# A softmax division moved to each head's output, in an attention stage of a two-layer kernel

## The chip, the cores and the metric

The kernel runs on one core of a Trainium2 chip. The metric is the device time of one execution in microseconds (us). Engines: TensorE (PE, its weight loads PEld), VectorE (DVE), ScalarE (ACT), GpSimd (POOL), and the sync engine SyncE (SP), which issues DMAs.

## The reference

Two layers on x of 2 x 512 x 1024. The first is cross attention with 32 query heads and 8 key/value heads of width 128 over a context of 2 x 1024 x 1024; behind it come a routed bias, a fake-quantised product and a gated feed-forward net. Only the attention's core is touched by the change:

```python
q = _apply_rope(q, curr_seq_pos)
k = _apply_rope(k, curr_seq_pos)
raw = jnp.einsum('bhqd,bhkd->bhqk', q, k) / scale
masked = raw + mask[:bs, None, curr_seq_pos:curr_seq_pos + sq, :sk]
attn = jax.nn.softmax(masked, axis=-1)
out = jnp.einsum('bhqk,bhkd->bhqd', attn, v)
out = out.transpose((0, 2, 1, 3)).reshape(bs, sq, N_Q_HEADS * D_V)
return out @ wo
```

Shapes here: 2 batches, 512 queries, 1024 keys.

## The kernel before

The program is a row of stages with a barrier between them: projections of queries, keys and values into DRAM (`q_d`, `k_d`, `v_d`), then `attention_stage`, which writes each head's transposed output to `o_d`, then `output_stage` and the rest. The change edits `attention_stage` alone, apart from one scratch array that `build` hands to it.

The stage walks over 2 batches x 32 heads x 4 quarters of 128 queries: 256 steps. Step n of the text is one quarter; four steps are a head, 16 steps a group of four heads that share a K and a V tile. All fp32 products are done as three products of high and low halves (`split_matmul`, L117 to L119), so that every operand is there as a high half (copied by ScalarE) and a low half (raw minus high: by GpSimd for Q, K, V, tiles at_ql, at_kl, at_vl; by VectorE for the probabilities, at_ptl).

Each engine has its own program, written out by hand, with the same loop: in step n it does the actions of the steps n minus a lag.

- TensorE: scores of step n (6 matmuls into at_s), transposes of step n-2 (8 into at_t, L1001), a quarter of the mixing with V of step n-6 (6 matmuls into at_o).
- VectorE: in step n `mask_and_max` (a memset of at_turnstile, then the fused add of the mask and row maximum, at_sc<-at_s, L952, then the negation, L955); for step n-1 `normalise` (reciprocal, L959, and the multiplication of the 128x1024 probabilities at_pr in place, L961); for step n-2 `turn_low` (at_ptl, L968, twice 128x512).
- ScalarE: the high halves of Q, K, V when due, `turn_high` of step n-2 (at_pth, L905), the exponential of step n with its row sum (at_pr, L895), and per head `copy_out` (at_ot<-at_o, L911) in step 4h+10 and `store_out` (a DMA to `o_d`, L916) in step 4h+11.
- GpSimd: the low halves of Q (step 4h-3), K (8 steps ahead of its group) and V (6 steps ahead).
- SyncE: the loads of Q, K and V at the same step numbers, each after a wait that its raw buffer is free.

The first LEAD = 12 steps are written out; then, for each batch, a loop of three passes over 32 steps, and the fourth pass written out again. So there are four returns of a loop in the stage, and each engine has its own.

Buffers: two each for at_s, at_sc, at_pr and at_ot; at_t has two halves, one for each four transposes. TensorE's transposes of step n-2 wait for `normed` (L961's event) and for the half of at_t to be free, which at_ptl of the step before frees.

Of the kernel before, what the change touches and what calls it, by code (L numbers as in the profile page):

```python
# [19 lines left out]
F32 = mybir.dt.float32  # L20
# [5 lines left out]
P = 128  # L26
# [7 lines left out]
QT = SQ // P  # L34
# [683 lines left out]
def attention_stage(nc, q_d, k_d, v_d, o_d, mask, ident):  # L718
# [8 lines left out]
    with ExitStack() as ctx:  # L727
# [18 lines left out]
        sm = sb("sm", [P, 2, 4], F32)  # L746
        turnstile = sb("turnstile", [P, 1], F32)
# [7 lines left out]
        o_st = [sem("o_st0"), sem("o_st1")]  # L755
        k_hi, v_hi, q_hi = event("k_hi"), event("v_hi"), event("q_hi")
# [4 lines left out]
        maxed = event("maxed")  # L761
        expd = event("expd", 2)
        recipd = event("recipd")
        normed = event("normed")
# [16 lines left out]

        def at(b, i, h):

            if isinstance(i, int):
                return b + (i * HP + h) // HQ, (i * HP + h) % HQ
            return b, i * HP + h

        MIX_LAG = QT + 2
        COPY_LAG = MIX_LAG + QT
        STORE_LAG = COPY_LAG + 1  # L790
        LEAD = STORE_LAG + 1

# [24 lines left out]
        def _(sp):  # L817
            def fetch(b, i, kind, x):
# [5 lines left out]
                elif kind == "v":  # L824
                    bb, h = at(b, i, x * GRP)
                    start = h // GRP * DH if isinstance(i, int) else i * (KG * DH) + x * DH
                    sp.wait_ge(v_lo.sem, v_lo.free(group(b, i, x), 1))
                    sp.dma_start(vraw[:], v_d[bb].rearrange("t p n -> p t n")[:, :, bass.ds(start, DH)]).then_inc(v_in, 16)
                else:
                    bb, h = at(b, i, x)  # L830
                    sp.wait_ge(q_lo.sem, q_lo.free(head(b, i, x), 2))
                    sp.dma_start(qraw[:, x % 2], q_d[bass.ds(h, 1)].rearrange("a p n -> p (a n)")[:, bb * SQ:(bb + 1) * SQ]).then_inc(q_in[x % 2], 16)

            def do_step(b, i, n):
                for kind, x in fetches(b, i, n):
                    fetch(b, i, kind, x)


# [8 lines left out]
            program(sp, do_step)  # L847

        @block.gpsimd
        def _(pool):  # L850
# [10 lines left out]

            def do_step(b, i, n):
                for kind, x in fetches(b, i, n):
                    fetch(b, i, kind, x)

            k_lo.open(pool)
# [7 lines left out]
        def _(act):  # L874
# [38 lines left out]
            def store_out(b, i, h):  # L913
                bb, hh = at(b, i, h)
                act.wait_ge(copied.sem, copied.done(head(b, i, h)))
                act.dma_start(o_d[bass.ds(hh, 1)].rearrange("a p n -> p (a n)")[:, bb * SQ:(bb + 1) * SQ],  # L916
                              ot[:, h % 2]).then_inc(o_st[h % 2], 16)

            def do_step(b, i, n):
# [6 lines left out]
                for lag, act_on in ((COPY_LAG, copy_out), (STORE_LAG, store_out)):  # L926
                    if (n - lag) % QT == 0 and exists(b, i, n - lag):
                        act_on(b, i, (n - lag) // QT)
# [3 lines left out]
            for s in range(2):  # L932
                act.sem_inc(o_st[s], 16)
# [3 lines left out]
            for s in range(2):  # L937
                act.wait_ge(o_st[s], 16 * (B * HQ // 2 + 1))

        @block.vector  # L940
        def _(dve):
            def mask_and_max(b, i, n):
# [3 lines left out]
                elif b == 0 and isinstance(i, int) and i == PASSES - 1 and n == NS:  # L946
# [28 lines left out]
            masked.open(dve)  # L975
            t_lo.open(dve)
# [3 lines left out]
        def _(pe):  # L980
# [14 lines left out]
            def turn(b, i, n):  # L995
                pe.wait_ge(normed.sem, normed.done(step(b, i, n)))
# [862 lines left out]
def build(nc, x, context, mask, wq, wk, wv, wo, router_w, router_b, expert_b, s1, z1, s2, z2,  # L1859
# [6 lines left out]
    v_d = scratch("v_d", (B, KT, P, D))  # L1866
    o_d = scratch("o_d", (HQ, DH, T))
# [31 lines left out]
    with ExitStack() as ctx:  # L1899
# [21 lines left out]
        attention_stage(nc, q_d, k_d, v_d, o_d, mask, ident)  # L1921
# [45 lines left out]
```

## Time and profile before

| | us |
|---|---|
| median of 3 runs | 3474.62 |
| lowest and highest run | 3468.10, 3477.11 |
| the profiled execution | 3472.4 |
| its span | 3470.6 |
| attention stage in it, about | 1000 to 1973 |

The page's first part, busy time, share of the span and instructions of each engine:

```profile
PE 3020.7 (87%) x14144; PEld 2418.9 (70%) x14144; DVE 2881.7 (83%) x4335; ACT 2154.2 (62%) x2742; POOL 911.7 (26%) x547
```

How to read the rows further below. In the view of stretches the columns are: the stretch, its length, then PE, PEld, DVE, ACT, POOL busy us with the number of instructions, the granted TensorE clock as a share of full speed, the DMA share, GB/s. In a timeline a row is: start us, duration us, engine, line, operation, written tile<-read tiles, shapes, how many were merged, and in brackets the engine's idle time ahead of it with what ended it. In the view of a line or tile: how many, duration in ns as min/median/max, first and last start. In the view of waits: who waited for whom, us in total, times, the longest. "issue" is time in which the engine waited for nothing that the profile shows. Ends of matmuls are modelled, and they are pipelined.

### The profile page before, as it was taken

What the parts mean: (1) busy time and instruction counts of PE and PEld (TensorE: products, weight loads), DVE (VectorE), ACT (ScalarE), POOL (GpSimd) and SP (SyncE); (2) the same over time, 40 slices, a digit from 0 to 9 for tenths busy, and PEclk for the clock granted to TensorE, in tenths of its full rate; (3) what the DMA queues carried; (4) which work ended last, traced back from release to release, by engine and by line L of the source; (5) the groups of instructions that cost most, each with busy time, mean ns of one, the idle gap of its engine ahead of it and who ended that gap; (6) DMA issues with size and microseconds to landing.
All of it is one profiled execution on the core that took longest, in us unless ns stands there. A gap on an engine that the chain in (4) does not pass through costs nothing. (4 is left out here: it accounts for less than half of the span.)

```text
span 3470.6 us, 45684 instructions
## 1 busy us (share of the span) xinstructions
PE 3020.7 (87%) x14144; PEld 2418.9 (70%) x14144; DVE 2881.7 (83%) x4335; ACT 2154.2 (62%) x2742; POOL 911.7 (26%) x547
## 2 busy tenths in 40 slices
PE   5888858687769999999999799995656999999999
PEld 4777746566648888888888677774425777777787
DVE  7999969679769999999999799997574788888753
ACT  4777747567657777777777588884142565655531
POOL 3777746226121111111111055550000101101100
PEclk8999979899989999999999899997577999999999
DMA  3333432342331111111111233420022221212211
GB/s 110 128 113 116 132 133 91 123 138 91 127 119 56 55 52 55 46 62 49 58 49 49 103 122 121 133 97 31 0 97 66 68 67 61 85 61 67 73 49 52
DMA packets 170400, 286.81 MB, mean 83 GB/s; under 512 B 11776, under 2 KB 98816, under 8 KB 170240
## 3 DMA queue, kind: packets, MB, share of 16 engines
q1 hardware_dynamic: 161024, 268.24, 23.3%
q10 hardware_dynamic: 9216, 16.78, 1.3%
q8 instruction: 58, 0.95, 0.1%
q14 instruction: 102, 0.84, 0.1%
HBM read 196.64 MB, written 88.34 MB: 82 GB/s over the span
## 5 line engine op out<-in xcount | busy, mean ns | idle before, releaser
L905 ACT ACTIVATE at_pth<-at_t 128x512 fp32r<-128x512 f32 x512 | 281.9, 596 | 249.3 <-PE at_t L1001 249.3
L205 ACT ACTIVATE ff_nf_above<-ff_nf_raw,sharp 128x1024 f32<-128x1024 f32 x255 | 291.6, 1148 | 92.5 <-DVE ff_nf_val L220 72.9
L952 DVE CUSTOM_DVE_ANT_0 at_sc<-at_s,at_mk 128x1024 f32<-128x1024 f32 x256 | 312.1, 1219 | 29.9 <-issue 9.5
L968 DVE TENSOR_TENSOR at_ptl<-at_t,at_pth 128x512 fp32r<-128x512 f32 x512 | 328.1, 682 | 1.1 <-ACT at_pth L905 1.1
L220 DVE SCALAR_TENSOR_TENSOR ff_nf_val<-ff_nf_above,ff_nf_val 128x1024 f32<-128x1024 f32 x238 | 308.2, 1295 | 21.2 <-ACT ff_nf_above L205 18.6
L205 ACT ACTIVATE pq_nf_above<-pq_nf_raw,sharp 128x1024 f32<-128x1024 f32 x240 | 263.2, 1113 | 99.3 <-DVE pq_nf_val L220 84.0
L205 ACT ACTIVATE ou_nf_above<-ou_nf_raw,sharp 128x1024 f32<-128x1024 f32 x240 | 267.3, 1117 | 77.8 <-DVE ou_nf_val L220 62.4
L895 ACT ACTIVATE at_pr<-at_sc,at_sm 128x1024 f32<-128x1024 f32 x256 | 295.3, 1154 | 14.7 <-DVE at_sm L955 7.9
L1001 PE MATMUL at_t<-ident,at_pr 128*128 128x128 f32 x2048 | 272.5, 274 | 20.1 <-DVE at_ptl L968 19.0
L117 PE MATMUL ff_g<-yT_h,ff_guh 128*128 128x512 f32 x704 | 286.6, 407 | 0.0
L1001 PEld LDWEIGHTS at_t<-ident,at_pr 128*128 128x128 f32 x2048 | 234.7, 140 | 71.4 <-DVE at_ptl L968 27.8
L220 DVE SCALAR_TENSOR_TENSOR pq_nf_val<-pq_nf_above,pq_nf_val 128x1024 f32<-128x1024 f32 x224 | 274.3, 1224 | 8.6
L220 DVE SCALAR_TENSOR_TENSOR ou_nf_val<-ou_nf_above,ou_nf_val 128x1024 f32<-128x1024 f32 x224 | 273.2, 1220 | 5.8
L119 PE MATMUL ff_g<-yT_h,ff_gul 128*128 128x512 f32 x704 | 276.3, 392 | 0.0
L118 PE MATMUL ff_g<-yT_l,ff_guh 128*128 128x512 f32 x704 | 274.6, 390 | 0.0
L117 PE MATMUL pq_pj<-xT_h,pq_wh 128*128 128x512 f32 x512 | 209.6, 409 | 55.5 <-POOL pq_wl L483 55.5
L117 PE MATMUL ou_acc<-ou_wh,ou_oh 128*128 128x512 f32 x512 | 210.4, 411 | 36.2 <-DVE X L1168 18.1
L860 POOL TENSOR_TENSOR at_ql<-at_qraw,at_qh 128x512 fp32r<-128x512 f32 x64 | 82.0, 1281 | 573.1 <-ACT at_qh L890 573.1
L961 DVE TENSOR_SCALAR at_pr<-at_pr,at_sm 128x1024 f32<-128x1024 f32 x256 | 218.8, 855 | 9.1
L117 PE MATMUL at_s<-at_kh,at_qh 128*128 128x512 f32 x512 | 201.7, 394 | 25.3 <-POOL at_ql L860 25.3
L117 PE MATMUL at_o<-at_pth,at_vh 128*128 128x512 f32 x512 | 221.8, 433 | 0.2 <-DVE at_ptl L968 0.2
L197 POOL TENSOR_TENSOR ff_nf_raw<-ff_nf_raw,ff_nf_am 128x1024 f32<-128x1024 f32 x17 | 39.5, 2321 | 690.5 <-DVE ff_nf_am L192 690.5
(210 smaller groups left out, 8105.5 us busy)
## 6 DMA issues: line engine op xcount, KB each, us to landing
ff_raw<-dq SPq DMA_DIRECT2D x63, 512.0 KB, 4.0
pq_raw<-in_L_xattn_wq SPq DMA_DIRECT2D x32, 512.0 KB, 5.1
q_d<-pq_res SPq DMA_DIRECT2D x32, 512.0 KB, 2.6
at_qraw<-q_d SPq DMA_DIRECT2D x64, 256.0 KB, 2.7
o_d<-at_ot ACTq DMA_DIRECT2D x64, 256.0 KB, 2.0
ou_oraw<-o_d SPq DMA_DIRECT2D x32, 512.0 KB, 3.8
ou_wraw<-in_L_xattn_wo SPq DMA_DIRECT2D x32, 512.0 KB, 4.1
pq_nf_raw<-in_L_ffn_w SPq DMA_DIRECT2D x16, 512.0 KB, 5.4
```

Of the source, the lines that this page charges most:

```text
L117: pe.matmul(out, w[0], x[0], start=start, stop=False)
L118: pe.matmul(out, w[0], x[1], start=False, stop=False)
L119: return pe.matmul(out, w[1], x[0], start=False, stop=stop)
L205: act.activation(self.above[:, (s + j) % 2, 0:width], self.raw[:, s, 0:width], ACT.Relu, bias=self.sharp[:, j:j + 1], scale=SHARP).then_in ...
L220: dve.scalar_tensor_tensor(v, above, STEPS[j], v, ALU.min, ALU.add).then_inc(self.stepped.sem, 1)
L860: pool.tensor_tensor(qq[1][:, x % 2], qraw[:, x % 2], f32(qq[0][:, x % 2]), ALU.subtract).then_inc(q_lo.sem, 1)
L895: act.activation(pr[:, n % 2], sc[:, n % 2], ACT.Exp, bias=sm[:, n % 2, 1:2], accum_out=sm[:, n % 2, 2:3]).then_inc(expd.sem, 1)
L905: act.activation(pt[0][:, h % 2, j * HALF:(j + 1) * HALF, (n % QT) * P:(n % QT + 1) * P], t_ps[:, j], ACT.Copy).then_inc(t_hi.sem, 1)
L952: dve.tensor_tensor_reduce(sc[:, n % 2], s_ps[:, n % 2], mk[:, bb * QT + n % QT], 1.0, NEG, ALU.add, ALU.max, sm[:, n % 2, 0:1]).then_inc( ...
L961: dve.tensor_scalar(pr[:, n % 2], pr[:, n % 2], sm[:, n % 2, 3:4], None, ALU.mult).then_inc(normed.sem, 1)
L968: dve.tensor_tensor(pt[1][sl], t_ps[:, j], f32(pt[0][sl]), ALU.subtract).then_inc(t_lo.sem, 1)
L1001: last = pe.transpose(t_ps[:, j, c, :], pr[:, n % 2, k * P:(k + 1) * P], ident[:])
```

## The change

The probabilities are no longer divided by their row sum before they are transposed. The exponential's row sums of a head's four quarters are gathered in `sums`; once per head VectorE inverts them (128x4) and transposes the inverses in blocks of 32x32 (`invert`). SyncE writes them to a small DRAM array `r_d` with four DMAs (`store_inverse`) and reads them back as one row of 512 for all 128 partitions (`load_inverse_row`); GpSimd multiplies the head's output at_ot by that row in place (`scale_out`), and SyncE, no longer ScalarE, stores it. The fused operation of the mask now makes the negated masked scores and their minimum, so that the negation of the maximum is gone, and the exponential takes a scale of -1. The transposes wait for `expd` instead of `normed`. In SyncE's order the stores of the inverses stand 8 steps, the row load 10 and the output's store 15 behind a head's first step; at the same step number the Q, K and V loads come first. LEAD is 16.

```diff
@@ attention_stage @@
-        sm = sb("sm", [P, 2, 4], F32)
-        turnstile = sb("turnstile", [P, 1], F32)
+        low = sb("low", [P, 2], F32)
+        sums = sb("sums", [P, 2, QT], F32)
+        inv = sb("inv", [P, 2, 32], F32)
+        invT = sb("invT", [P, 2, 32], F32)
+        inv_row = sb("inv_row", [P, 2, SQ], F32)
+        turnstile = sb("turnstile", [P, 2], F32)
...
-        STORE_LAG = COPY_LAG + 1
+        STORE_LAG = COPY_LAG + QT + 1
         LEAD = STORE_LAG + 1
+        INV_LAG = QT
+
+        INV_OUT_LAG = 2 * QT
+        ROW_LAG = INV_OUT_LAG + 2
...
+            def store_inverse(b, i, h):
+
+                sp.wait_ge(inv_turned.sem, inv_turned.done(head(b, i, h)))
+                for q in range(P // 32):
+                    sp.dma_start(r_d[h % 2].rearrange("(t q j) -> q t j", t=QT, j=32)[q],
+                                 invT[32 * q:32 * q + QT, h % 2]).then_inc(inv_out[h % 2], 16)
+
+
+            def load_inverse_row(b, i, h):
+                sp.wait_ge(inv_out[h % 2], written(b, i, h) + 64)
+                sp.dma_start(inv_row[:, h % 2], r_d[h % 2].rearrange('(a n) -> a n', a=1).broadcast_to((P, SQ))).then_inc(inv_in[h % 2], 16)
+
+            def store_out(b, i, h):
+                bb, hh = at(b, i, h)
+                sp.wait_ge(scaled.sem, scaled.done(head(b, i, h)))
+                sp.dma_start(o_d[bass.ds(hh, 1)].rearrange("a p n -> p (a n)")[:, bb * SQ:(bb + 1) * SQ],
+                             ot[:, h % 2]).then_inc(o_st[h % 2], 16)
+
             def do_step(b, i, n):
                 for kind, x in fetches(b, i, n):
                     fetch(b, i, kind, x)
-
+                for lag, act_on in ((INV_OUT_LAG, store_inverse), (ROW_LAG, load_inverse_row), (STORE_LAG, store_out)):
+                    if (n - lag) % QT == 0 and exists(b, i, n - lag):
+                        act_on(b, i, (n - lag) // QT)
...
+            def scale_out(b, i, h):
+                pool.wait_ge(inv_in[h % 2], passed(b, i, h) + 16)
+                pool.wait_ge(copied.sem, copied.done(head(b, i, h)))
+                pool.tensor_tensor(ot[:, h % 2], ot[:, h % 2], inv_row[:, h % 2], ALU.mult).then_inc(scaled.sem, 1)
+
             def do_step(b, i, n):
+                if (n - COPY_LAG) % QT == 0 and exists(b, i, n - COPY_LAG):
+                    scale_out(b, i, (n - COPY_LAG) // QT)
                 for kind, x in fetches(b, i, n):
                     fetch(b, i, kind, x)
...
             def exponentials(b, i, n):
-                act.wait_ge(maxed.sem, maxed.done(step(b, i, n)))
+                h, quarter = n // QT, n % QT
+                if quarter == 0:
+
+                    act.wait_ge(inverted.sem, inverted.free(head(b, i, h), 2))
+                act.wait_ge(masked.sem, masked.done(step(b, i, n)))
                 act.wait_ge(turned.sem, turned.free(2 * step(b, i, n) + 1, 4))
-                act.activation(pr[:, n % 2], sc[:, n % 2], ACT.Exp, bias=sm[:, n % 2, 1:2],
-                               accum_out=sm[:, n % 2, 2:3]).then_inc(expd.sem, 1)
+                act.activation(pr[:, n % 2], sc[:, n % 2], ACT.Exp, bias=low[:, n % 2:n % 2 + 1], scale=-1.0,
+                               accum_out=sums[:, h % 2, quarter:quarter + 1]).then_inc(expd.sem, 1)
...
-                dve.memset(turnstile[:], 0.0)
-                dve.tensor_tensor_reduce(sc[:, n % 2], s_ps[:, n % 2], mk[:, bb * QT + n % QT], 1.0, NEG,
-                                         ALU.add, ALU.max, sm[:, n % 2, 0:1]).then_inc(masked.sem, 1)
-                dve.wait_ge(masked.sem, masked.done(step(b, i, n)))
-                dve.tensor_scalar(sm[:, n % 2, 1:2], sm[:, n % 2, 0:1], -1.0, None, ALU.mult).then_inc(maxed.sem, 1)
-
-            def normalise(b, i, n):
-                dve.wait_ge(expd.sem, expd.done(step(b, i, n)))
-                dve.reciprocal(sm[:, n % 2, 3:4], sm[:, n % 2, 2:3]).then_inc(recipd.sem, 1)
-                dve.wait_ge(recipd.sem, recipd.done(step(b, i, n)))
-                dve.tensor_scalar(pr[:, n % 2], pr[:, n % 2], sm[:, n % 2, 3:4], None, ALU.mult).then_inc(normed.sem, 1)
+                dve.memset(turnstile[:, n % 2:n % 2 + 1], 0.0)
+                dve.tensor_tensor_reduce(sc[:, n % 2], s_ps[:, n % 2], mk[:, bb * QT + n % QT], -1.0, -NEG,
+                                         ALU.add, ALU.min, low[:, n % 2:n % 2 + 1]).then_inc(masked.sem, 1)
+
+            def invert(b, i, h):
+                dve.wait_ge(expd.sem, expd.done(step(b, i, QT * (h + 1) - 1)))
+                dve.reciprocal(inv[:, h % 2, 0:QT], sums[:, h % 2]).then_inc(inverted.sem, 1)
+                dve.wait_ge(inverted.sem, inverted.done(head(b, i, h)))
+                dve.wait_ge(inv_out[h % 2], written(b, i, h))
+                dve.transpose(invT[:, h % 2], inv[:, h % 2]).then_inc(inv_turned.sem, 1)
...
             def do_step(b, i, n):
-                for lag, act_on in ((0, mask_and_max), (1, normalise), (2, turn_low)):
-                    if exists(b, i, n - lag):
-                        act_on(b, i, n - lag)
+                if exists(b, i, n):
+                    mask_and_min(b, i, n)
+                if (n - INV_LAG) % QT == 0 and exists(b, i, n - INV_LAG):
+                    invert(b, i, (n - INV_LAG) // QT)
+                if exists(b, i, n - 2):
+                    turn_low(b, i, n - 2)
...
             def turn(b, i, n):
-                pe.wait_ge(normed.sem, normed.done(step(b, i, n)))
+                pe.wait_ge(expd.sem, expd.done(step(b, i, n)))
```

## Rows read from the trace of the kernel before

**Rows 1.** Stretches: most of the stage, then two plain steps.
```profile
1050.00:1950.00 900.00, 888.03 (x4838) 741.76 (x4837) 844.97 (x1937) 650.15 (x1117) 144.21 (x88) 1.00 0.15 52
1380.39:1384.00 3.61, 3.61 (x22) 3.08 (x21) 3.40 (x8) 2.85 (x5) 0.24 (x1) 1.00 0.00 0
1299.31:1302.96 3.65, 3.65 (x22) 3.08 (x21) 3.41 (x9) 2.81 (x5) 0.00 (x0) 1.00 0.30 120
```

**Rows 2.** The timeline of one plain step, at_sc to at_sc.
```profile
1380.39 1.22 DVE L952 CUSTOM_DVE_ANT_0 at_sc<-at_s,at_mk 128x1024 f32<-128x1024 f32 x1
...
1380.81 1.09 ACT L905 ACTIVATE at_pth<-at_t 128x512 fp32r<-128x512 f32 x2 [1.26 <-PE at_t L1001]
...
1381.91 0.75 DVE L961 TENSOR_SCALAR at_pr<-at_pr,at_sm 128x1024 f32<-128x1024 f32 x1
1381.92 1.15 ACT L895 ACTIVATE at_pr<-at_sc,at_sm 128x1024 f32<-128x1024 f32 x1
...
1382.58 1.28 DVE L968 TENSOR_TENSOR at_ptl<-at_t,at_pth 128x512 fp32r<-128x512 f32 x2
...
1384.00 1.22 DVE L952 CUSTOM_DVE_ANT_0 at_sc<-at_s,at_mk 128x1024 f32<-128x1024 f32 x1
```

**Rows 3.** Timeline of a step in which GpSimd splits K.
```profile
1153.77 1.22 DVE L952 CUSTOM_DVE_ANT_0 at_sc<-at_s,at_mk 128x1024 f32<-128x1024 f32 x1
...
1153.95 2.41 POOL L854 TENSOR_TENSOR at_kl<-at_kraw,at_kh 128x1024 fp32r<-128x1024 f32 x1 [9.98 <-ACT at_kh L880]
...
1155.29 1.62 DVE L961 TENSOR_SCALAR at_pr<-at_pr,at_sm 128x1024 f32<-128x1024 f32 x1
...
1156.84 1.27 DVE L968 TENSOR_TENSOR at_ptl<-at_t,at_pth 128x512 fp32r<-128x512 f32 x2
...
1157.57 0.66 PE L1001 MATMUL at_t<-ident,at_pr 128*128 128x128 f32 x4 [0.24 <-DVE at_ptl L968]
1158.04 1.21 DVE L952 CUSTOM_DVE_ANT_0 at_sc<-at_s,at_mk 128x1024 f32<-128x1024 f32 x1
```

**Rows 4.** The view of one line: L961, L968 and L952.
```profile
L961 DVE TENSOR_SCALAR at_pr<-at_pr,at_sm x256: 752/754/1665, 1011.5 to 1959.3; 128x1024 f32<-128x1024 f32 x128
...
L968 DVE TENSOR_TENSOR at_ptl<-at_t,at_pth x512: 673/682/693, 1017.1 to 1963.0; 128x512 fp32r<-128x512 f32 x171
...
L952 DVE CUSTOM_DVE_ANT_0 at_sc<-at_s,at_mk x256: 1211/1220/1226, 1007.7 to 1955.7; 128x1024 f32<-128x1024 f32 x128
```

**Rows 5.** The waits of the stretch 1050 to 1950, TensorE's row.
```profile
PE at_t L1001 <- DVE at_ptl L968: 12.0, 32, 1.5
```

**Rows 6.** The timeline around a return of the loop over passes.
```profile
1165.92 1.21 DVE L952 CUSTOM_DVE_ANT_0 at_sc<-at_s,at_mk 128x1024 f32<-128x1024 f32 x1
...
1168.10 1.28 DVE L968 TENSOR_TENSOR at_ptl<-at_t,at_pth 128x512 fp32r<-128x512 f32 x2
...
1171.53 0.06 DVE L951 MEMSET at_turnstile<- 128x1 f32 x1 [2.15 <-issue]
...
1174.54 0.66 PE L1001 MATMUL at_t<-ident,at_pr 128*128 128x128 f32 x4 [1.49 <-DVE at_ptl L968]
...
1175.01 1.22 DVE L952 CUSTOM_DVE_ANT_0 at_sc<-at_s,at_mk 128x1024 f32<-128x1024 f32 x1
```

**Rows 7.** The timeline of the stage's start, VectorE.
```profile
1018.36 1.22 DVE L952 CUSTOM_DVE_ANT_0 at_sc<-at_s,at_mk 128x1024 f32<-128x1024 f32 x1
...
1021.75 1.22 DVE L952 CUSTOM_DVE_ANT_0 at_sc<-at_s,at_mk 128x1024 f32<-128x1024 f32 x1
```

**Rows 8.** The timeline of the stage's end.
```profile
1958.71 1.17 PE L1001 MATMUL at_t<-ident,at_pr 128*128 128x128 f32 x8 [0.82 <-DVE at_ptl L968]
...
1970.11 0.34 ACTq L916 DMA_DIRECT2D o_d<-at_ot  x1
```

**Rows 9.** The view of the tile at_ql, GpSimd's row of it.
```profile
L860 POOL TENSOR_TENSOR at_ql<-at_qraw,at_qh x64: 1264/1283/1293, 1003.3 to 1933.7; 128x512 fp32r<-128x512 f32 x64
```

**Rows 10.** The view of the tile at_qraw: landings of its loads.
```profile
DMA to landing us min/median/max: 2.5/2.7/13.2
```

More of the change, by code:

```diff
@@ L755, in attention_stage @@
         o_st = [sem("o_st0"), sem("o_st1")]
+        inv_out = [sem("inv_out0"), sem("inv_out1")]
+        inv_in = [sem("inv_in0"), sem("inv_in1")]
         k_hi, v_hi, q_hi = event("k_hi"), event("v_hi"), event("q_hi")
@@ L760, in attention_stage @@
         masked = event("masked", 2)
-        maxed = event("maxed")
         expd = event("expd", 2)
-        recipd = event("recipd")
-        normed = event("normed")
+        inverted = event("inverted", 2)
+        cleared = sem("cleared")
+        inv_turned = event("inv_turned")
+        scaled = event("scaled", 2)
         turned = event("turned", 4)
@@ L780, in step, with passed @@
             return i * NS + (b * HQ * QT + n)
+        def passed(b, i, h):
+            return i * (16 * HP // 2) + 16 * (b * HQ // 2 + h // 2)
         def at(b, i, h):
@@ L786, in at, with written @@
             return b, i * HP + h
+        def written(b, i, h):
+            return i * (64 * HP // 2) + 64 * (b * HQ // 2 + h // 2 + 1)
         MIX_LAG = QT + 2
         COPY_LAG = MIX_LAG + QT
-        STORE_LAG = COPY_LAG + 1
+        STORE_LAG = COPY_LAG + QT + 1
         LEAD = STORE_LAG + 1
+        INV_LAG = QT
+        INV_OUT_LAG = 2 * QT
+        ROW_LAG = INV_OUT_LAG + 2
         def exists(b, i, n):
@@ L825, in fetch @@
                     bb, h = at(b, i, x * GRP)
-                    start = h // GRP * DH if isinstance(i, int) else i * (KG * DH) + x * DH
+                    start = h // GRP * DH if isinstance(i, int) else (i * KG + x) * DH
                     sp.wait_ge(v_lo.sem, v_lo.free(group(b, i, x), 1))
@@ L836, in do_step @@
                     fetch(b, i, kind, x)
+                for lag, act_on in ((INV_OUT_LAG, store_inverse), (ROW_LAG, load_inverse_row), (STORE_LAG, store_out)):
+                    if (n - lag) % QT == 0 and exists(b, i, n - lag):
+                        act_on(b, i, (n - lag) // QT)
+            for s in range(2):
+                sp.sem_inc(o_st[s], 16)
+                sp.sem_inc(inv_out[s], 64)
             tiles = mask.rearrange("b (t p) k -> p (b t) k", p=P)
@@ L847, in _ @@
             program(sp, do_step)
+            for s in range(2):
+                sp.wait_ge(o_st[s], 16 * (B * HQ // 2 + 1))
         @block.gpsimd
@@ L911, in copy_out @@
                 act.activation(ot[:, h % 2], o_ps[:, h % 2], ACT.Copy).then_inc(copied.sem, 1)
[L913 to L917, printed above, removed]
             def do_step(b, i, n):
@@ L925, in do_step @@
                     exponentials(b, i, n)
-                for lag, act_on in ((COPY_LAG, copy_out), (STORE_LAG, store_out)):
-                    if (n - lag) % QT == 0 and exists(b, i, n - lag):
-                        act_on(b, i, (n - lag) // QT)
+                if (n - COPY_LAG) % QT == 0 and exists(b, i, n - COPY_LAG):
+                    copy_out(b, i, (n - COPY_LAG) // QT)
             expd.open(act)
             copied.open(act)
-            for s in range(2):
-                act.sem_inc(o_st[s], 16)
             for kind, x in FIRST:
@@ L936, in _, with mask_and_min @@
             program(act, do_step)
-            for s in range(2):
-                act.wait_ge(o_st[s], 16 * (B * HQ // 2 + 1))
         @block.vector
         def _(dve):
-            def mask_and_max(b, i, n):
+            def mask_and_min(b, i, n):
                 bb = at(b, i, n // QT)[0]
@@ L970, in do_step @@
             def do_step(b, i, n):
-                for lag, act_on in ((0, mask_and_max), (1, normalise), (2, turn_low)):
-                    if exists(b, i, n - lag):
-                        act_on(b, i, n - lag)
+                if exists(b, i, n):
[4 more added lines that the diff above has]
+                    turn_low(b, i, n - 2)
             masked.open(dve)
+            inverted.open(dve)
+            dve.memset(inv[:], 0.0).then_inc(cleared, 1)
+            dve.wait_ge(cleared, 1)
             t_lo.open(dve)
@@ L1866, in build @@
     v_d = scratch("v_d", (B, KT, P, D))
+    r_d = scratch("r_d", (2, SQ))
     o_d = scratch("o_d", (HQ, DH, T))
```

5 lines of the change are left out of this document (3 added, 2 removed).

## The prediction

> **What bounds the kernel now.** I read the slices of the page first: the attention stage runs from about 1000 to 1973 us, and no other stage is edited, so what is asked is what ends last inside one of its 256 steps. The view of stretches answers for the whole: from 1050 to 1950 TensorE is busy 888.0 of 900 us, VectorE 845.0, ScalarE 650.2, GpSimd 144.2, at a granted clock of 1.00, the upper level of 2.4 GHz [rows 1]. The same view of one plain step has TensorE busy in all 3.61 us of it (3.65 us in another, whose matmuls simply come a little wider apart) [rows 1]. So a plain step is paced by TensorE, whose work the change doesn't touch, and VectorE, at 3.40 of 3.61 us, is close behind but not the bound.
>
> The loss lies in the steps that are not plain. In the view of the line, at_sc starts 256 times between 1007.7 and 1955.7 [rows 4]: 255 distances make 948.0 us, where 255 x 3.61 = 920.6. The surplus of 27.4 us is what a perfect cover of VectorE could give back between these two starts. Two kinds of step hold nearly all of it:
>
> Steps with a K or V split. The reader is to see that the normalisation at_pr (L961) takes 1.62 us while GpSimd works on at_kl for 2.41 us, that at_ptl behind it starts late, and that TensorE's transposes then wait for at_ptl [rows 3]. The step is 4.27 us long instead of 3.61. L961 has a median of 754 ns and a longest of 1665; at_ptl (673 to 693) and at_sc (1211 to 1226) never stretch, whatever GpSimd does [rows 4]. A stretched step comes for each K and each V tile, 15 times two behind the first.
>
> Returns of the loop over passes, four of them. VectorE stands still for 2.15 us with no releaser but "issue" before its memset, and the wait at the transposes is 1.49 us [rows 6]. TensorE's own stream shows no such hole there.
>
> The waits agree in number: TensorE waited for at_ptl 32 times, 12.0 us in all, in the stretch that holds 14 of the 15 pairs and the four returns [rows 5]. A wait is shorter than the step's excess because that view shows the modelled end of the matmuls; I price by distances of at_sc.
>
> **The change, part by part.** *VectorE, per step.* Gone are L961 (0.75 us), the reciprocal and the negation of the maximum, which becomes a scaled minimum in the same fused operation as before. at_ptl (1.28 us for its two halves) starts 2.19 us behind at_sc [rows 2]; it could now start as soon as at_sc is through, 1.22 us and some 0.1 behind its start. I take 1.35: that is 0.84 us earlier. The remaining chain of a step is 1.35 + 1.28 = 2.63 us, which leaves 0.98 us of 3.61 free. In a plain step this gives nothing, because TensorE paces it: next late is TensorE itself.
>
> *Split steps.* No operation is left on VectorE that was ever seen to stretch. Excess of the K step 4.27 - 3.61 = 0.66 us [rows 3]; the V step of the same pair is like it. 15 x 2 x 0.66 = 19.8 us at most; where the plain steps run at 3.65 a pair is worth some 0.1 us less. I take 19.0, with 15 as the lower end (a little of the delay could also be ScalarE's K and V copies) and 19.8 as the upper.
>
> *Returns.* The two distances from 1165.92 to 1175.01 make 9.09 us, against 2 x 3.61: 1.87 us per return, 7.5 for four [rows 6]. Afterwards the 2.15 us stand behind an at_ptl that ends at 2.63 instead of at 3.46: at_sc starts at about 4.8 rather than 5.65, and at_ptl behind it 0.84 us closer. Together at_ptl is 1.7 us earlier against a wait of 1.49 [rows 6], so TensorE wouldn't wait, with 0.2 us in hand. That is narrow, and one of the four may cost more: I take 7.0, with 0 and 7.5 as ends. LEAD grows from 12 to 16 steps, so the returns come four steps later (ahead of steps 48 and 80 of each batch, not 44 and 76); they stay clear of the K and V splits.
>
> *Start and end.* In the first steps there is no mixing yet, TensorE is light and VectorE paces: 3.39 us a step [rows 7]. With 2.63 us of VectorE these few go to some 2.7: three steps of 0.7, about 2.0 us. At the end the wait of 0.82 us at the last transposes but one [rows 8] goes too, but the last output now takes GpSimd's multiplication before its store. Its nearest row is the 128x512 subtraction at 1.28 us [rows 9]; with a hand-over of 0.1 that is +1.4 - 0.9, net +0.4 or so. I keep -0.5 and +1.4 as ends, the upper if nothing of the tail shortens.
>
> *ScalarE.* The exponential has the same shape and starts behind at_pth anyway (1.51 us behind at_sc's start, and it starts at 1.53 [rows 2]), so that the shorter way to its bias gives nothing. It loses 64 store issues of 0.34 us [rows 8], which nobody waited for: 0.
>
> *VectorE, per head.* A reciprocal of 128x4 and a 32x32-block transpose, 64 times, unseen in this trace. The nearest row for small work is the memset at 0.06 us, for large work at_ptl's half at 0.68 [rows 4, 6]; two of them and a wait between lie between 0.2 and 1.5 us, nearer to the lower because they are 4 and 32 columns wide. I take 0.5. It stands ahead of at_ptl once in four steps and fits into the 0.98 us free: 0, and 0.5 us x 64 only if that cover is gone.
>
> *GpSimd, per head.* 64 x 1.28 = 82 us more [rows 9], on an engine busy for 144 of 900 [rows 1]. Its multiplication is queued ahead of the V split of the same step and waits for the head's copy-out at the step's end, so V's low half comes about 4 us later; its first reader is 12 steps (43 us) away. K's and Q's splits stand in other steps. 0.
>
> *SyncE's queue.* Per head it gets four small stores, a row load, and the output store. The moved Q, K and V loads are now behind waits: the load of Q for head h+3 stands behind the stores of head h's inverses, which are ready in step 4h+4, and is needed in step 4h+9, some 18 us later. From those take 2 us on VectorE, five issues of 0.34 us and a landing of 2.7 us [rows 8, 10]: 11 us are left. K and V stand behind the output store of two heads earlier and have over 3 steps. Because stores and row loads stand four steps later in this order, nothing here waits for work that isn't a head old: 0.
>
> **Sum.** 19.0 + 7.0 + 2.0 - 0.4 = 27.6 us off. The profiled execution took 3472.4 us (its span 3470.6), so 3444.8. The median of the three runs is 3474.6, 2.2 us more, by which it is 3447.0. I give **3446**.
>
> **The Trainium skill against the trace.** Rows 3 and 4 show L961 stretched and two operations with one operand in PSUM not. The Trainium skill, SBUF — State Buffer, section "Who interferes with whom", has VectorE and GpSimd take turns at one pair of ports: a VectorE operation in a two-port mode, or one with two SBUF inputs against a GpSimd operation that reads SBUF, blocks wholly, and others don't. The trace agrees (1.62 us against 0.75). By that rule all of the split steps' excess goes and GpSimd's new work costs VectorE nothing; without it, each of 64 multiplications might hold VectorE as at_kl did, for 0.87 us, which the free 0.98 us would still hide.
>
> **Rivals.**
> *A: the split steps stay long.* Were it ScalarE's K and V copies that delay at_pth, only returns and edges would be gained: 8.6 us, 3465. Against it: in rows 3 it is L961 that stretches, and at_ptl starts right behind it. 0.07.
> *B: the returns keep their price,* since ScalarE and TensorE return too, and once VectorE is early the next of them is late, or the 0.2 us in hand are not there. 20.6 us, 3453. For it: only one engine's hole can be seen at a time. 0.15.
> *C, the slower side: SyncE's queue becomes the bound.* Place: the row load's wait for four stores of 128-byte pieces, ahead of every later load. A head lasts 4 x 3.61 = 14.4 us; seven issues are 2.4 us, so it decides once these stores take more than 12.0 us to land; each further us costs 64. The longest landing in rows 10 is 13.2: (13.2 - 12.0) x 64 - 27.6 = +49, 3523. It is slower than before by over 0.3% from 12.6 us on. Against it: the median of rows 10 is 2.7, and 13.2 is from the stage's first loads beside the masks. 0.04.
> *D: TensorE's pace.* If all steps come 3.65 us apart, as in the second plain step [rows 1], up to 256 x 0.04 = 10 us are lost, less what such steps already cost in the trace (their share of the 27.4): some 7, 3453. 0.08.
> *E: the change doesn't do what it says,* for instance the new minimum form of the fused operation being longer than 1.22 us. Up to 0.98 us more is hidden, twice the length would give a VectorE step of 3.85 us: +0.24 x 256 - 27.6 = +34, 3508. 0.02.
>
> **How the numbers follow.** The forecast, with its own range from 3438 to 3451, has 0.64. The runs of before spread from 3468 to 3477, which alone is 4.5 us either way. The range takes in B and D, the lower end of the split steps (4 us) and that spread, not A, C and E: 3436 to 3460, which leaves out A, C, E and some of the forecast's edge, under 2 in 10. About 0.3% (10.4 us) is what a measurement of this kernel can tell from no change. Faster by more: forecast, B, D, and a little of A: 0.88; within: most of A, 0.06; slower: C and E, 0.06.
>
> **What would show it.** L961 gone; distances of at_sc of 3.61 to 3.65 us in the steps with at_kl and at_vl; VectorE idle about 1 us a step "<- PE at_s"; the waits of TensorE for at_ptl nearly gone; from 1050 to 1950 VectorE busy about 2.75/3.61 of the time and TensorE over 99%; SyncE's Q loads landing before step 4h+9. The prediction is wrong if TensorE's waits name expd, q_lo or at_ptl as often as before, if a hole stays at the returns, or if a later stage has another length.

## The result and the profile after

| | before | after |
|---|---|---|
| median of 5 runs each | 3474.78 | 3456.68 |
| lowest and highest | 3468.10, 3477.11 | 3454.3, 3462.1 |
| the profiled execution, its span | 3472.4, 3470.6 | 3454.41, 3452.5 |

The ratio is 0.995, interval 0.9936 to 0.9965: faster by 18 us, where 28 were forecast. Two executions on record stand far off the rest, one of 6187 us of experiment 11's kernel and one of 7773 us of the kernel before beside experiments 5 to 8; no ratio contains them. The page's first part of the kernel after has 639 VectorE instructions fewer and 64 more on GpSimd:

```profile
PE 3017.7 (87%) x14144; PEld 2431.6 (70%) x14144; DVE 2626.0 (76%) x3696; ACT 2140.3 (62%) x2742; POOL 996.1 (29%) x611
```

The view of stretches over 880 us of the attention stage (columns as ahead of [rows 1]), and from the waits of the same stretch the largest ones:

```profile
1050.00:1930.00 880.00, 880.00 (x4874) 750.01 (x4874) 615.98 (x1341) 642.58 (x1125) 222.22 (x149) 1.00 0.22 71
...
POOL at_ot L910 <- ACT at_ot L968: 371.0, 61, 13.2
POOL at_ql L905 <- ACT at_qh L943: 248.0, 60, 6.0
ACT at_pth L962 <- PE at_t L1052: 236.8, 243, 1.5
DVE at_turnstile L997 <- PE at_s L119: 172.0, 144, 1.3
DVE at_sc L998 <- issue: 85.3, 99, 1.2
```

TensorE is busy in all 880.00 us, and the view has no wait of it any more, where [rows 5] had 32 for at_ptl. VectorE is down from 94% [rows 1] to 70% and waits for TensorE's scores. In the stage TensorE is the only bound that is left.

A step with GpSimd's K split, in the timeline, and the line of at_sc:

```profile
1149.79 1.22 DVE L998 CUSTOM_DVE_ANT_0 at_sc<-at_s,at_mk 128x1024 f32<-128x1024 f32 x1
1149.80 2.41 POOL L899 TENSOR_TENSOR at_kl<-at_kraw,at_kh 128x1024 fp32r<-128x1024 f32 x1 [2.72 <-ACT at_kh L933]
1150.94 0.17 DVE L1003 RECIPROCAL at_inv<-at_sums 128x4 f32<-128x4 f32 x1
1151.15 0.21 DVE L1006 STREAM_TRANSPOSE at_invT<-at_inv 128x32 f32<-128x32 f32 x1
1151.29 1.26 DVE L1013 TENSOR_TENSOR at_ptl<-at_t,at_pth 128x512 fp32r<-128x512 f32 x2
...
1153.26 1.22 DVE L998 CUSTOM_DVE_ANT_0 at_sc<-at_s,at_mk 128x1024 f32<-128x1024 f32 x1 [0.71 <-issue]
...
L998 DVE CUSTOM_DVE_ANT_0 at_sc<-at_s,at_mk x256: 1219/1224/1225, 1007.8 to 1926.5; 128x1024 f32<-128x1024 f32 x128
```

The step is 3.47 us long (the steps of a head alternate around 3.61), not 4.27 as in [rows 3], although the same 2.41 us of GpSimd lie in it; and it holds the reciprocal and the transpose too. The 255 distances of at_sc make 918.7 us, against 948.0 in [rows 4].

By its kinds of step the gain of 29.3 us is: 1.8 over the first six distances; 19.0 over 45 steps at the splits (the K step, the next and the V step of 15 pairs, as they are numbered before); 7.6 over the eight steps at the four returns (the one with the return and the one behind it); 0.8 over the rest.

At a return itself the prediction had VectorE's hole of 2.15 us stay and be covered, with at_sc about 4.8 us behind the last one. The first return of the kernel after, which lies between at_ptl and the memset:

```profile
1175.09 1.23 DVE L998 CUSTOM_DVE_ANT_0 at_sc<-at_s,at_mk 128x1024 f32<-128x1024 f32 x1
...
1176.24 1.28 DVE L1013 TENSOR_TENSOR at_ptl<-at_t,at_pth 128x512 fp32r<-128x512 f32 x2
1178.66 0.06 DVE L997 MEMSET at_turnstile<- 128x1 f32 x1 [1.14 <-PE at_s L119]
1178.70 1.23 DVE L998 CUSTOM_DVE_ANT_0 at_sc<-at_s,at_mk 128x1024 f32<-128x1024 f32 x1
```

The distance is 3.61 us, and VectorE is idle for 1.14 us, as in the plain step before it; it is the same at the other three. So the hole isn't covered: it is gone, or shorter than 1.14 us.

**Stage by stage,** by first and last starts of the rows that open and close each, before to after, the change in us: at_sc 948.0 to 918.7 (-29.3); from there to the output stage's first load 17.0 to 17.4 (+0.4); the output stage, up to the load of the router's weights, 441.9 to 444.7 (+2.8); from there to the first ro_tmp 17.7 in both; the router stage, which adds the routed bias, from that ro_tmp on 65.0 to 71.3 (+6.3); the query stage behind it 105.9 to 107.2 (+1.3); from there to the feed-forward net 44.2 to 45.6 (+1.4); the net 820.2 to 819.0 (-1.1). These make -18.2, which is the difference of the spans within 0.1. So attention gave 28.9 us, and 10.7 came back in stages whose code is the same. Two places of that can be seen.

In the output stage, VectorE has two holes, one at each of the two returns of its loop, that the waits of before don't have. From the waits and the timeline of after:

```profile
DVE X L1219 <- issue: 3.6, 2, 1.8
...
2063.28 2.47 DVE L220 SCALAR_TENSOR_TENSOR ou_nf_val<-ou_nf_above,ou_nf_val 128x1024 f32<-128x1024 f32 x2
2067.53 0.69 DVE L1219 TENSOR_TENSOR X<-ou_acc,X 128x512 f32<-128x512 f32 x1 [1.78 <-issue]
```

Between the same two waits of TensorE on either side of a hole lie 50.9 us after and 49.7 and 49.8 before, so the holes make 2.3 of the 2.8 us.

In the router stage it is TensorE's clock. First before: the views of the lines of its first and last VectorE operation and three stretches; then the same of after, from the same point of the stage on.

```profile
L1333 DVE SCALAR_TENSOR_TENSOR ro_tmp<-xn,ro_sm,X x8: 1277/1278/1279, 2432.3 to 2492.5; 128x1024 f32<-128x1024 f32 x8
L1335 DVE TENSOR_TENSOR X<-ro_m,ro_tmp x8: 1224/1225/1225, 2436.4 to 2497.3; 128x1024 f32<-128x1024 f32 x8
...
2430.00:2440.00 10.00, 8.71 (x53) 7.11 (x51) 5.71 (x23) 2.06 (x6) 0.00 (x0) 0.87 0.00 0
2440.00:2450.00 10.00, 9.25 (x32) 6.46 (x33) 5.20 (x13) 2.80 (x6) 0.00 (x0) 0.65 0.00 0
2450.00:2460.00 10.00, 9.64 (x31) 6.63 (x30) 4.03 (x12) 1.62 (x4) 0.00 (x0) 0.50 0.01 2
```

```profile
L1384 DVE SCALAR_TENSOR_TENSOR ro_tmp<-xn,ro_sm,X x8: 1277/1278/1280, 2406.3 to 2472.8; 128x1024 f32<-128x1024 f32 x8
L1386 DVE TENSOR_TENSOR X<-ro_m,ro_tmp x8: 1224/1225/1226, 2413.3 to 2477.6; 128x1024 f32<-128x1024 f32 x8
...
2404.00:2414.00 10.00, 9.64 (x33) 6.75 (x32) 3.58 (x12) 1.62 (x4) 0.00 (x0) 0.50 0.00 0
2414.00:2424.00 10.00, 9.64 (x33) 6.75 (x32) 4.48 (x14) 1.62 (x4) 0.00 (x0) 0.50 0.00 0
2424.00:2434.00 10.00, 9.64 (x33) 6.75 (x33) 4.39 (x16) 1.64 (x5) 0.00 (x0) 0.50 0.01 2
```

The granted clock is the third number from the right: 0.50 is the level of 1.2 GHz. Before, it rose for about ten us at the stage's start (53 matmuls in 8.71 busy us) and fell back; after, it stays low from the first matmul, with TensorE 96% busy in these stretches.

### The profile page after: what moved, and what is told of

Read it like the earlier page. It is cut to its first block and busy times, and to the rows that moved or that the text cites. A ratio compares the mean times of both kernels' runs of the same rounds, so it can differ in the third digit from the quotient of the medians.

```text
span 3452.5 us, 45501 instructions
## 1 busy us (share of the span) xinstructions
PE 3017.7 (87%) x14144; PEld 2431.6 (70%) x14144; DVE 2626.0 (76%) x3696; ACT 2140.3 (62%) x2742; POOL 996.1 (29%) x611
## 5 line engine op out<-in xcount | busy, mean ns | idle before, releaser
L952 ACT ACTIVATE at_pr<-at_sc,at_low 128x1024 f32<-128x1024 f32 x256 | 295.1, 1153 | 0.6 <-DVE at_inv L1003 0.4
L220 DVE SCALAR_TENSOR_TENSOR pq_nf_val<-pq_nf_above,pq_nf_val 128x1024 f32<-128x1024 f32 x224 | 274.3, 1224 | 8.6
L118 PE MATMUL pq_pj<-xT_l,pq_wh 128*128 128x512 f32 x512 | 206.6, 403 | 0.0
L119 PE MATMUL pq_pj<-xT_h,pq_wl 128*128 128x512 f32 x512 | 205.9, 402 | 0.0
```

Of the source, the lines that this page charges most:

```text
L118: pe.matmul(out, w[0], x[1], start=False, stop=False)
L119: return pe.matmul(out, w[1], x[0], start=False, stop=stop)
L220: dve.scalar_tensor_tensor(v, above, STEPS[j], v, ALU.min, ALU.add).then_inc(self.stepped.sem, 1)
L952: act.activation(pr[:, n % 2], sc[:, n % 2], ACT.Exp, bias=low[:, n % 2:n % 2 + 1], scale=-1.0, accum_out=sums[:, h % 2, quarter:quarter + ...
```

## The experiments

**The theory:** the gain is VectorE's L961 in the split steps and VectorE's shorter chain at the returns; what came back is the router's clock and the holes, neither of them work of the change. **The rivals:** any VectorE work less would have done it (then it is not the kind of operation that L961 is); the four steps of later order on SyncE are worth nothing, as I had costed them; the give-back is the stages' own length in another run, or is caused by the moment at which they start.

**1. L961 alone.** In the kernel before the multiplication is left out, so the probabilities are never divided and the output is not the softmax's:

```diff
-                dve.reciprocal(sm[:, n % 2, 3:4], sm[:, n % 2, 2:3]).then_inc(recipd.sem, 1)
-                dve.wait_ge(recipd.sem, recipd.done(step(b, i, n)))
-                dve.tensor_scalar(pr[:, n % 2], pr[:, n % 2], sm[:, n % 2, 3:4], None, ALU.mult).then_inc(normed.sem, 1)
+                dve.reciprocal(sm[:, n % 2, 3:4], sm[:, n % 2, 2:3]).then_inc(normed.sem, 1)
```

> The kernel before without the multiplication L961 (the division of the softmax is left out; all the rest, the row sums and their reciprocals too, as before). Theory 1 (the normalisation on VectorE is what stretches the steps and bares the loop's returns): the distance from the first to the last at_sc falls from 948.0 us to 918 to 923, as in the changed kernel (918.7), and TensorE has next to no waits for at_ptl. Rival (the output side of the change, SyncE's and GpSimd's new work, has a part in the gain): it stays above 930. For the whole kernel: the stage gives some 28 us; if what was given back behind the stage in the changed kernel hangs on when the later stages start, the total gain here can be anything from 18 to 30 us, and the router's stage is 65 or 71 us long; if it hangs on the change's new code, it is 65 us long and the gain is 28.

Median 3446.45, ratio to before 0.9918 (0.9897 to 0.994). The stretch and the line of at_sc:

```profile
1050.00:1930.00 880.00, 877.46 (x4821) 741.73 (x4820) 636.65 (x1688) 645.31 (x1113) 144.46 (x88) 1.00 0.16 53
...
L952 DVE CUSTOM_DVE_ANT_0 at_sc<-at_s,at_mk x256: 1219/1220/1227, 1008.0 to 1935.9; 128x1024 f32<-128x1024 f32 x128
```

927.9 us, between the two expectations. By its distances every K and V step is plain (3.61 or 3.65 us) with GpSimd's splits in place, so L961 alone made the split steps. The whole difference, 948.0 - 927.9 = 20.1, is not the split steps' alone: the 45 steps at the splits give 18.0, the first six distances 2.0, the eight steps at the returns 2.6, and the rest takes back 2.6. The four returns stay long, at 4.78, 5.00, 4.72 and 5.10 us: with a plain step of 3.65 taken off each, 5.0 in all. VectorE still has the reciprocal and the negation, and stands still for 2.0 to 2.4 us ahead of its memset at each. Of the 9.2 us to the kernel after the returns make 5.0, and pace nearly all else: 147 steps come 3.65 us apart. The four runs spread from 3440.5 to 3458.47, and the profiled one is the slowest of them, so what follows rests on its distances and not on its median.

**2. SyncE's order.** In the kernel after, stores and row loads four steps earlier:

```diff
-        STORE_LAG = COPY_LAG + QT + 1
+        STORE_LAG = COPY_LAG + 1
-        INV_OUT_LAG = 2 * QT
+        INV_OUT_LAG = QT
```

> The changed kernel with SyncE's stores of inverses, row loads and output stores four steps earlier in its order (lags 4, 6 and 11 instead of 8, 10 and 15, LEAD 12). Theory 1 (order matters): the load of Q for head h+4, at step 4h+13, stands behind the stores of head h+2's inverses, which VectorE has ready only in step 4h+12. 2 us on VectorE, five issues of 0.34 us and a landing of 2.8 us put it some 3 to 4 us behind ScalarE's need; ScalarE then holds up at_pth and TensorE by 1.5 to 3.5 us per head: 62 heads make 90 to 220 us, so 3550 to 3680 us. Rival (SyncE has slack enough in any order): within 10 us of the changed kernel's 3457.

3535.48, ratio 1.018 (1.0155 to 1.0205); 78.8 us above the kernel after, with 83.6 more between the first and last at_sc (1002.3). That is 1.3 us a head, and under the expectation's 1.5 to 3.5 us and 3550 to 3680, though far beyond the rival's 10 us. Its waits from 1050 to 1930, and one head in the timeline:

```profile
ACT at_qh L943 <- DMA at_qraw<-q_d: 161.3, 55, 4.0
DVE at_ptl L1013 <- ACT at_pth L962: 157.1, 82, 3.5
PE at_t L1052 <- DVE at_ptl L1013: 47.9, 65, 2.4
...
1246.48 0.21 DVE L1006 STREAM_TRANSPOSE at_invT<-at_inv 128x32 f32<-128x32 f32 x1
...
1246.72 1.27 SPq L857 DMA_DIRECT2D r_d<-at_invT  x4
...
1248.25 0.37 SPq L851 DMA_DIRECT2D at_qraw<-q_d  x1
...
1251.23 0.63 ACT L943 ACTIVATE at_qh<-at_qraw 128x512 fp32r<-128x512 f32 x1 [3.60 <-DMA at_qraw<-q_d]
```

The chain can be read off: the Q load stands in SyncE's order behind a store that waits for this step's transpose, lands 3 us later, ScalarE waits for it in its own order with at_pth behind, at_ptl waits for at_pth and TensorE for at_ptl, once a head. In the kernel after the same load stands behind stores whose data is a head old; ScalarE waited for a Q load once (3.0 us). So the order is a part of this change, without which it would be a loss of some 60 us against before.

**3. and 4. Put VectorE's work back, in two kinds.** In the kernel after, each step, where L961 stood:

```diff
+                    for x in range(2):
+                        dve.wait_ge(spared.sem, spared.free(2 * step(b, i, n - 1) + x, 1))
+                        dve.tensor_scalar(spare[:], mk[:, 0, x * 512:(x + 1) * 512], 0.5, None, ALU.mult).then_inc(spared.sem, 1)
```

> The changed kernel with idle work put back on VectorE where L961 stood: per step two multiplications 128x512, both operands in SBUF, of the same kind as L961 (about 0.8 us), read by nobody. Theory 1 (GpSimd's K and V splits hold up this kind of operation): steps with a K or V split are long again; with the four returns the distance from first to last at_sc is 940 to 950 us instead of 918.7, and the idle operation takes over 1 us in some 30 steps. Rival (it is VectorE's time alone): no stretched operation, and the same distance as in e4_one_port.

```diff
+                    dve.wait_ge(spared.sem, spared.free(step(b, i, n - 1), 1))
+                    dve.tensor_reduce(spare[:, 0:1], mk[:, 0, 0:680], AX.X, ALU.max).then_inc(spared.sem, 1)
```

> The changed kernel with idle work of about 0.8 us per step in the same place, but of a kind with a single SBUF input and a result of one column (a maximum over 128x680). Theory 1: no step with a K or V split is long; only the returns of the loop, which VectorE's free time covered, cost again, up to 1.9 us each: first to last at_sc 918 to 927 us. Rival (VectorE's time alone makes the split steps long): 940 or more, as in e3_two_port.

The first: 3493.86, ratio 1.0067 (1.0049 to 1.0085), at_sc 965.9. The second: 3463.51, ratio 0.9974 (0.9959 to 0.9989), at_sc 931.0. The lines of the two added operations, a V step of the first between them:

```profile
L1025 DVE TENSOR_SCALAR at_spare<-at_mk x512: 382/426/2503, 1010.2 to 1976.4; 128x512 f32<-128x512 f32 x171
...
1166.16 1.27 POOL L912 TENSOR_TENSOR at_ot<-at_ot,at_inv_row 128x512 f32<-128x512 f32 x1 [6.74 <-ACT at_ot L970]
...
1167.39 2.41 POOL L904 TENSOR_TENSOR at_vl<-at_vraw,at_vh 128x1024 fp32r<-128x1024 f32 x1
1167.74 2.81 DVE L1025 TENSOR_SCALAR at_spare<-at_mk 128x512 f32<-128x512 f32 x2
1170.46 1.28 DVE L1015 TENSOR_TENSOR at_ptl<-at_t,at_pth 128x512 fp32r<-128x512 f32 x2
1171.20 1.25 PE L1059 MATMUL at_t<-ident,at_pr 128*128 128x128 f32 x8 [1.18 <-DVE at_ptl L1015]
```

```profile
L1024 DVE TENSOR_REDUCE at_spare<-at_mk x256: 816/856/862, 1011.3 to 1942.0; 128x1 f32<-128x680 f32 x128
```

The same order of VectorE time a step (0.88 and 0.86 us), and the one stretches (30 of its 512 take over 1 us) while the other never does. So it is the kind of operation and not VectorE's time; the two kinds differ in more than one thing, the width of the result too, and which of these counts the runs don't separate. The multiplications cost 965.9 - 918.7 = 47.2 us, with K steps of 4.24 to 4.31, V steps of 5.07 to 5.23 and returns of 4.78 to 5.42. I had expected 940 to 950: the V split now starts right behind GpSimd's new multiplication, 0.35 us ahead of VectorE's pair, which took 2.81 us instead of 0.88; a K split starts 1.52 us ahead of it, and there the pair took 1.62. In both the pair ends 0.75 us behind the split. The reduction has no stretched split step; its 931.0 lie above the expected 918 to 927, with two returns of 4.83 and 4.81 us, each with a step over 4.1 behind it, and the pace of 3.65 in many steps.

These runs say something on the returns too. In experiment 4 the first two cost nothing, with VectorE idle for 0.41 us there, and the last two have holes of 1.6 us; in experiment 1, where at_ptl starts 1.40 us behind at_sc against 1.92 in 4, so that VectorE has more time in hand, all four have them. So the hole comes and goes from kernel to kernel, and that a shorter chain on VectorE covers it is shown by no run.

**5. and 6. The two kernels again, unedited.**

> The changed kernel once more, unedited, for its trace. Theory 2 (10 us of the stage's 29 were given back because TensorE's clock in the router's stage falls out by the moment at which the stage begins): the attention stage repeats (first to last at_sc 918 to 929 us, by TensorE's pace of 3.61 or 3.65 us a step), while the router's stage may be anything from 55 to 72 us long. Rival (the change makes the router's stage longer): it is 71.3 us again, as in its first trace.

> The kernel before once more, unedited. Theory 2: first to last at_sc 945 to 952 us; the router's stage anything from 55 to 72 us. Rival: the router's stage is 65.0 us again.

3454.2 and 3472.81, one execution each. The router stage takes 71.3 and 64.9 us, the output stage 444.8 and 442.8: nearly the lengths of the first profiles. So as far as two traces of each can tell, the give-back belongs to the kernel, and not to one run of it.

**7., 9. and 10. The moment at which the stage starts.** In the kernel after, idle GpSimd memsets of 951 ns each, in a stage of their own between the output stage and the norm ahead of the router: 6, 14 and 30.

```diff
+        pause_stage(nc, 6)
         with ExitStack() as c:
```

> The changed kernel with a pause ahead of the first layer's router part: GpSimd fills 128x1024 six times between two barriers, and nothing else runs; at 0.96 us each and a barrier that is 6 to 8 us. Theory 2: the router's stage begins so much later and its length may come out at another value than 71.3 us (50 to 72), with the granted clock in it to match. Rival (a cost of the change's code): 71.3 us, and the whole 6 to 8 us longer than without the pause.

> The changed kernel with the pause of e7_pause at 14 fills instead of 6, some 12.3 us where that gave 5.1. Theory 2 in its sharper form (the router stage's length goes by the moment at which it starts): its first ro_tmp comes at about 2419 us, where e4_one_port's came, so the stage is about 61 us long, 10 less than the changed kernel's 71.3, and the total is only some 2 us above the changed one, 3454 to 3460 us. Rival (the length belongs to the change's code): 71.3 us, total 3466 to 3470 us.

> The changed kernel with 30 fills, some 26.7 us. Theory 2: the first ro_tmp comes at about 2433 us, where the kernel before had it (2432.3 and 2433.0), so the stage is about 65 us long as there. Total 3472 to 3478 us. Rival: 71.3 us, total 3480 or more.

3460.22, 3465.97 and 3488.33, one execution each. The router's first ro_tmp starts at 2412.4, 2419.5 and 2440.6, and the stage takes 71.3, 71.4 and 71.3 us. The second of these starts within 0.4 us of where it starts in experiment 4 (2419.1), whose router takes 61.1 us; experiment 3's takes 55.8. Both expected lengths, 61 and 65 us, were wrong. The third was aimed at the moment of the kernel before, 2432.3, and missed it by 8 us. Counted from the program's start, the moment alone does not decide.

The traces hold a regularity that none of these runs was made for. Behind the output stage TensorE stands idle and the granted clock falls to 0.50. In the four traces in which it rose again in the router stage (both of before, experiments 3 and 4), that fall came 47.1 to 48.5 us ahead of the first ro_tmp, and the rise 47.8 us behind the fall in each; in the seven others the fall came 49.2 to 76.2 us ahead. So what decides may be how the stage's matmuls lie against moments of the clock that don't move with the program. The pauses weren't aimed at that, so this rival is untested and the cause stays open; that each unedited kernel had the same length twice is all that is known of repeating.

**8., 11. and 12. Hold the clock up.** Idle bf16 matmuls on TensorE, into a bank of their own: 16 ahead of the router's first transposes and 6 per tile of 128 rows. Runs 8 and 12 have them in the kernel after, 11 in the kernel before.

```diff
+            def keep_busy(count, first=False):
+                for x in range(count):
+                    pe.matmul(f_ps[:], fb[:, 0:P], fb[:], start=True, stop=True)
...
+            keep_busy(16, True)
...
+                keep_busy(6)
```

> The changed kernel with idle bf16 matmuls (128x128 by 512 columns, into a PSUM bank that nobody reads) in the router's stage: 16 ahead of its first transposes and 6 per tile where TensorE would wait for VectorE's choice. Theory 2 (the stage's length is TensorE's clock): granted clock 1.00 through most of the stage; a tile then takes some 6.4 us, as two of before's did, instead of 9.55, so the stage from the first ro_tmp to the last sum is 45 to 55 us long instead of 71.3, and the kernel is 12 to 25 us faster than the changed one: 3432 to 3448 us. Rival (the stage is bound by the chain over VectorE and ScalarE): nothing gained, or a few us lost to the fillers, 3457 to 3465.

> The kernel before with the idle matmuls of e8_filler in the router's stage. Theory 2: the granted clock stays high there as well, so the stage is 50 us long in both, and the change is then worth what the attention stage gives (29 us) less some 2 to 3 us in the output stage: this kernel is 24 to 30 us above e8_filler's, some 3460 to 3464 us. Rival (the change costs the router's stage 6 us by its code): it stays 18 us above e8_filler, some 3453.

> The kernel of e8_filler once more, so that e11_before_filler is compared with it on the same chip. 3427 to 3441 us, the router's stage 50 us long.

After with filler: 3435.08, ratio to before 0.9872 (0.9847 to 0.9896), and again 3434.61, 0.9903 (0.9868 to 0.9938). Before with filler: 3457.86, 0.9959 (0.9945 to 0.9974), under the expected 3460 to 3464. The lines and two stretches of run 12, then the lines of run 11:

```profile
L1400 DVE TENSOR_TENSOR X<-ro_m,ro_tmp x8: 1225/1225/1225, 2409.1 to 2455.1; 128x1024 f32<-128x1024 f32 x8
...
2405.00:2415.00 10.00, 9.28 (x49) 5.27 (x47) 5.45 (x14) 2.80 (x6) 0.00 (x0) 1.00 0.00 0
2415.00:2425.00 10.00, 9.64 (x64) 6.80 (x62) 6.31 (x21) 2.06 (x6) 0.00 (x0) 1.00 0.01 2
```

```profile
L1349 DVE TENSOR_TENSOR X<-ro_m,ro_tmp x8: 1224/1225/1226, 2434.1 to 2480.6; 128x1024 f32<-128x1024 f32 x8
L952 DVE CUSTOM_DVE_ANT_0 at_sc<-at_s,at_mk x256: 1210/1220/1225, 1008.1 to 1956.1; 128x1024 f32<-128x1024 f32 x128
```

The clock is granted at 1.00 from 10 us ahead of the first ro_tmp to 48 us behind it, and the stage takes 50.0 us in run 12 and 50.5 in run 11, though more matmuls run in it. With that term equal on both sides the change is worth 3457.9 - 3434.6 = 23.3 us (24.6 by the spans), slightly under the 24 to 30 expected. The four runs of 12 spread over 8 us, so the totals alone hardly tell 23 from 18; the lengths of the stage do. So the 6.3 us of the router are its clock and not the change's work. Nor do they go with the change's code or its saving: experiment 1, in the code of before, has 71.3 too; experiment 2 has it and is slower than before; experiments 3 and 4, in the code of after, have 55.8 and 61.1. The kernel after with filler is the fastest of all here, 22 us below the kernel after. The output stage stays at 441.9 in run 11 and 444.7 in run 12: in every run, kernels with attention's old code have 441.9 to 442.8 and those with the new one 444.5 to 444.8 (the runs with a pause, which falls into this stretch, left aside). Why an unedited loop has holes at its returns in one of them wasn't found, and no run tests it.

## Why the prediction was right, and which step failed

The time, 3456.7, lies in the range and under the kernel before, but 10.7 us above the forecast, close to rivals B and D (3453), and through the mechanism of neither. Rivals A and E fell: the split steps are plain, and the new minimum form of the fused operation takes 1224 ns against 1220.

- **Split steps, 19.0:** right, 19.0 measured. Experiment 1 removes them with one operation. Experiments 3 and 4 show by what they put back that it is the kind of operation. The trace agrees with the port rule that the prediction weighed (the Trainium skill, SBUF — State Buffer, "Who interferes with whom"): multiplications in SBUF alone went from 0.75 to 1.62 us and from 0.88 to 2.81, while operations with an operand in PSUM, and the reduction, did not stretch at all.
- **Returns, 7.0:** right in size, 7.6, and not by the mechanism. No return costs TensorE anything after, and at_ptl starts 1.15 us behind at_sc, not 1.35. But the hole of 2.15 us was to stay and at_sc to come at 4.8 us; it came at 3.61, with at most 1.14 us of hole. The step that failed here is "Afterwards the 2.15 us stand behind an at_ptl that ends at 2.63". Why the hole is gone no run shows, and that it is gone was luck for this term: experiments 1 and 3 have it at all four returns, experiment 4 at two. Rival B didn't come about, but it wasn't put to the test either.
- **Start, 2.0:** 1.8. That is over the first six distances; three of them fall to 3.14, 2.95 and 2.58 us, from 3.39 in [rows 7].
- **Tail, +0.4:** +0.4, with a multiplication of 1283 ns.
- **Inverses, 0 on the path, 0.5 us a head on VectorE:** 0.17 and 0.21 us, hidden.
- **Pace:** outside the start, the splits and the returns 0.8 us were gained: before had 55 steps near 3.65 us and after has none. With the 0.6 more at the returns attention gave 28.9 us net against 27.6 forecast. Rival D was absent here, but run 8 shows it is real: the same kernel's at_sc take 928.1 us there and 919.9 in run 12.
- **SyncE's order, 0:** right for what was shipped, and reasoned thinly. That "nothing here waits for work that isn't a head old" is a condition worth 79 us, and the trace supported it only through the landing times. Rival C had the right place and the wrong price: the four stores take 1.27 us to issue, and a row load 2.9 to 5.0 us to land. What SyncE can cost is a wait in it ahead of the Q load, and not the stores' own time.
- **The step that failed in the total** is the premise of the first paragraph: "no other stage is edited, so what is asked is what ends last inside one of its 256 steps", and that the sum from there goes straight to the end. It doesn't: the router stage took 6.3 us more by its clock, the output stage 2.8 more with two holes, the stages between there and the feed-forward net 2.7 more, less 1.1 in the net. The last sentence of the prediction names the sign ("if a later stage has another length") and the sum gave it neither a term nor a rival. That the router's 6.3 us are its clock is shown by experiment; what makes the clock rise or stay, and what makes the holes, is open.

The forecast's own range, 3438 to 3451, was missed. The wide one held since B and D had put 3453 and the spread of the runs into it; neither of them is what happened, so that is luck.

## What to carry to other kernels

Price a step by the distances of one operation over the whole stage, split the surplus over the plain step into its kinds, and ask of each kind which single operation makes it: here that gave 19.0 of 29.3 us by a cause that the runs show. A hole with no releaser is not such a kind. It went at the returns of one stage (7.6 us) and came at those of another (2.3 us), and neither was worked out ahead; don't count on it either way. A store whose data is ready only now belongs behind the loads in a shared queue, however small it is; that order was worth more than four times the change. Leave room for stages that aren't edited, above all where TensorE runs at the lower clock in short matmuls, and look there for a gain of its own: 64 idle matmuls took 15.7 us off the kernel before, nearly as much as the change.

## What the runs showed of the hardware beyond that

- In one unedited stage, TensorE 96% busy by the profile in most of it, the granted clock stayed at 0.50 in seven traces (71.3 or 71.4 us) and rose for a part of it in four (65.0, 64.9, 61.1, 55.8); with idle bf16 matmuls it was at 1.00 for nearly all of it in three of three (50.0 to 50.5).
- How long a GpSimd split of 2.4 us holds a pair of VectorE multiplications goes by which starts when: 2.81 us where the pair was due 0.35 us behind the split's start, 1.62 where 1.52 us, 0.88 without one.
- At a granted clock of 1.00 a step's matmuls take 3.61 us in one execution and 3.65 in another of the same kernel, 8 us over the stage.
- A loop's return left VectorE idle for 1.9 to 2.15 us with no releaser at all four of the attention stage before [rows 6], at none of them after, and for 1.5 to 1.6 us at two of four in experiment 4. In the output stage it was 1.8 us at both returns after, and nothing before.
